# Attention values of two head pairs at once on TensorE, out projections in the steps between, and a reordered VectorE program

## The chip, the cores and the metric

The kernel runs on one core of a Trainium2 chip. A core has five engines that run their own instruction streams and meet at semaphores: TensorE (PE, matmuls and transpositions, with its weight loads shown as PEld), VectorE (DVE), ScalarE (ACT), GpSimd (POOL) and SyncE (SP, which issues most transfers). The metric is the device time of one execution in microseconds.

## What is computed

One decoder layer over 8 batches of 256 rows of width 128, in float32. Self-attention has 16 heads of 64, cross-attention one head over 512 context rows, and the feed-forward block quantises its inputs and weights.

```
x = x + _L0_attn_ref(_layernorm(x, axis=-1), L0_attn_norm_scale, L0_attn_wq, L0_attn_wk, L0_attn_wv, L0_attn_w_out, L0_attn_b_out)
x = x + _L0_xattn_ref(ctx_1024, ctx_1024, _layernorm(x, axis=-1), L0_xattn_Wk, L0_xattn_Wv, L0_xattn_bv, L0_xattn_Wq, L0_xattn_bq, L0_xattn_Wo, L0_xattn_bo)
x = x + _L0_ffn_ref(_layernorm(x, axis=-1), L0_ffn_w1, L0_ffn_b1, L0_ffn_w2, L0_ffn_b2)
...
weights = jnp.einsum('bqhd,bkhd->bhqk', q, kf)
weights = jax.nn.softmax(weights, axis=-1).astype(dtype)
new_vals = jnp.einsum('bhqk,bkhd->bqhd', weights, v).astype(dtype)
out = jnp.einsum('bqhe,hed->bqd', new_vals, w_out) + b_out
```

## The kernel before

The self-attention of a batch is done in eight steps, `j` = 0 to 7, one for each pair of heads. A step of one kind ("first" for batch 0, "mid" for batches 1 to 6 in a hardware loop over two batches at a time, "last" for batch 7) is written out by hand on each engine, in the function `step` of that engine, and semaphores tie the engines together. After the last batch come a tail and the feed-forward block. The order of the work is the order in which the code is written. Step `j` works at several pairs at once:

- TensorE projects queries and keys of pair `j + 3` (`project_qk`, called Q below, 6 matmuls), makes the scores of pair `j + 2` (`scores`, S, 12 matmuls), turns the two probability tiles of pair `j` (`turn_probs`, T0 and T1, 4 transpositions each), multiplies values and turned probabilities of pair `j - 1` (`values`, V, 4 matmuls that the profile records as 8) and projects the output of pair `j - 2` into `acc_bank` (`project_out`, P, 2 matmuls recorded as 4).
- ACT splits Q's result (`split_hi`, writes `q_hi`), takes the exponentials of the first and of the second head (`exps`), and copies V's result into `oT`.
- DVE takes the maxima of the scores (`maxima`, writes `negmax`), copies the two turned tiles into `pT` (`keep_turned`), makes the low part of the split (`split_lo`, `q_lo`), and inverts the row sums (`invert_sums`). GpSimd scales the probabilities (`scale_probs`).

Beside this each step has up to two side tasks, at the places `(j, 0)` and `(j, 1)` of a table. All share one PSUM bank, `side_bank`, so each waits until the one before has been copied out (`side_free`).

```
PLACE = {(0, 0): "W2", (0, 1): "TC", (1, 0): "W1", (2, 0): "W3", (2, 1): "TX", (3, 0): "QX", (3, 1): "TH",
         (4, 0): "SX0", (4, 1): "PX0", (5, 0): "SX1", (5, 1): "PX1", (6, 0): "UX", (6, 1): "OX", (7, 0): "V0"}
```

W0 to W3 and V0 project values, TC turns the context (`cT_hi`, `cT_lo`), TX the normalised rows of the cross-attention (`xn2`, made by DVE; its copies are `x2T_hi` and `x2T_lo`), TH the normalised rows of the next batch (`xn1`; `ht_hi`, `ht_lo`); QX makes the cross queries (`qx_hi`, `qx_lo`), SX0 and SX1 the cross scores (DVE `x_negmax`, then ACT `x_prob`), PX0 and PX1 turn their probabilities (ACT copies them into `x_pT`), UX and OX finish the cross-attention (`uT`, `x_all`). In every step TensorE writes the side task of the first place between Q and S, and that of the second between P and V. ACT takes the copy of the second place's task after the exponentials of the first head and before those of the second.

`turned_bank` is the single bank for T0 and T1, so T1 waits until DVE has copied T0, and T0 until it has copied the T1 before. The scores of step `j` wait until both heads' exponentials of step `j - 1` are out of the two score banks. `residual` in step 1 adds the projected output of the previous batch to its rows; `statistics`, `aggregate` and `normalise` are the three parts of a layer norm, whose inverse root is taken by GpSimd between the last two.

## Time and profile before

| | |
|---|---|
| time before, median of 3 runs | 398.27 us (397.82 to 398.81) |
| profiled execution, its own time | 397.71 us |
| its span (first to last instruction) | 395.9 us |
| TensorE busy | 379.5 us, 96% of the span |
| TensorE weight loads | 286.7 us, 72% |
| DVE busy | 324.5 us, 82% |
| ACT busy | 259.4 us, 66% |
| POOL busy | 163.8 us, 41% |
| granted TensorE clock | 0.999 of full speed |

The span runs from the first to the last instruction; the time of the execution holds 1.8 us more around it. A group of instructions is named by the line that issues it, its engine and what it writes and reads. Matmuls overlap each other, so the duration of one is longer than its distance to the next; a matmul in float32 is recorded as two.

### The profile page before, as it was taken

Reading aid. Unit: us, or ns where it says so; the run is one execution under the profiler, and the core shown is the slowest. Engines: PE = TensorE matmul, PEld = TensorE weight load, DVE = VectorE, ACT = ScalarE, POOL = GpSimd, SP = SyncE. Lnnn points to the kernel's source line nnn. Section 1 sums busy time; section 2 is a strip of 40 time slices with the busy share of each in tenths; the row PEclk is TensorE's granted clock in tenths of the full one; section 3 lists DMA queues with packets and bytes.
Section 4 is the critical chain, followed back from the end, with each engine's and each line's share of the span. In section 5 each row is a group of like instructions: output and inputs, shape, how many; then the busy total and the mean of one; then the engine's idle time right before and its main releaser. Section 6 shows DMA issues by size and latency. Waiting matters only on the chain.

```text
span 395.9 us, 9105 instructions
## 1 busy us (share of the span) xinstructions
PE 379.5 (96%) x3011; PEld 286.7 (72%) x3011; DVE 324.5 (82%) x777; ACT 259.4 (66%) x807; POOL 163.8 (41%) x179
## 2 busy tenths in 40 slices
PE   8999999999999999999999999999999999988975
PEld 8778777777777777777777777777777777766422
DVE  3988779869897889869895989869986998757994
ACT  4976676666667556767676656757675677725674
POOL 3665444524544345425454345444453444501000
PEclk9999999999999999999999999999999999999999
DMA  7500000001000100001000100001000000000003
GB/s 244 142 15 2 2 2 0 3 2 40 2 3 2 40 0 0 0 0 40 0 0 0 40 0 0 0 4 36 0 0 0 26 2 2 0 2 0 2 0 106
DMA packets 12310, 7.50 MB, mean 19 GB/s; under 512 B 1280, under 2 KB 11264, under 8 KB 12288
## 3 DMA queue, kind: packets, MB, share of 16 engines
q1 hardware_dynamic: 11856, 6.69, 5.7%
q10 hardware_dynamic: 432, 0.52, 0.4%
q8 instruction: 13, 0.21, 0.3%
q14 instruction: 9, 0.07, 0.1%
HBM read 6.16 MB, written 1.05 MB: 18 GB/s over the span
## 4 chain that ended last, share of the span: by engine, by line
PE 65%; DVE 18%; issue 10%; ACT 3%; DVEq 1%; POOL 1%; POOLq 0%; ACTq 0%
PE turned_bank L473 13%; PE o_bank L482 12%; PE score L463 12%; PE acc_bank L489 5%; DVE negmax L925 3%; DVE pT L932 3%; PE side_bank L446 3%; PE side_bank L540 3%; PE q_bank L446 3%; PE q_bank L448 3%; PE q_bank L447 3%; DVE h_max L1250 2%; PE side_bank L447 2%; PE side_bank L448 2%; ACT prob L746 2%
## 5 line engine op out<-in xcount | busy, mean ns | idle before, releaser
L1294 POOL TENSOR_TENSOR prob<-prob,rinv 128x512 f32<-128x512 f32 x128 | 132.6, 1044 | 146.6 <-DVE rinv L929 146.6
L746 ACT ACTIVATE prob<-score,negmax 128x256 f32<-128x256 f32 x252 | 117.6, 476 | 71.5 <-DVE negmax L925 69.7
L925 DVE TENSOR_REDUCE negmax<-score 128x2 f32<-128x512 f32 x126 | 85.9, 682 | 27.0 <-PE score L463 25.6
L932 DVE COPY pT<-turned_bank 128x512 f32<-128x512 f32 x124 | 84.2, 679 | 7.0 <-PE turned_bank L473 6.6
L473 PE MATMUL turned_bank<-ident,prob 128*128 128x128 f32 x496 | 81.0, 286 | 1.7 <-DVE pT L932 1.2
L473 PEld LDWEIGHTS turned_bank<-ident,prob 128*128 128x128 f32 x496 | 52.0, 141 | 33.6 <-issue 24.2
L482 PE MATMUL o_bank<-pT,v_sb 128*64 128x256 f32 x512 | 69.4, 392 | 0.6 <-ACT oT L737 0.6
L746 ACT ACTIVATION_READ_ACCUMULATOR prob<-score,negmax 128x1 f32 x252 | 51.3, 203 | 0.0
L482 PEld LDWEIGHTS o_bank<-pT,v_sb 128*64 128x64 f32 x512 | 31.1, 136 | 19.9 <-issue 8.2
L737 ACT ACTIVATE q_hi<-q_bank 128x512 fp32r<-128x512 f32 x63 | 38.2, 606 | 10.9 <-PE q_bank L448 10.0
L917 DVE TENSOR_TENSOR q_lo<-q_bank,q_hi 128x512 fp32r<-128x512 f32 x63 | 42.7, 680 | 0.0
L463 PE MATMUL score<-q_hi 64*128 64x256 f32 x252 | 42.2, 330 | 0.2
L446 PE MATMUL q_bank<-ht_hi,wqk_hi 128*128 128x256 f32 x126 | 40.9, 325 | 0.0
L1285 POOL TENSOR_TENSOR rstd<-veps,ln_pow 128x2 f32<-128x2 f32 x24 | 17.0, 710 | 53.5 <-DVE veps L948 52.8
L489 PE MATMUL acc_bank<-wo_sb,oT 128*128 128x128 f32 x256 | 39.0, 276 | 0.0
L463 PEld LDWEIGHTS score<-q_hi 64*128 64x128 f32 x252 | 23.7, 184 | 18.6 <-issue 15.4
L463 PE MATMUL score<-q_lo,q_hi 64*128 64x256 f32 x252 | 35.6, 277 | 0.0
L463 PE MATMUL score<-q_hi,q_lo 64*128 64x256 f32 x252 | 35.6, 277 | 0.0
L448 PE MATMUL q_bank<-ht_hi,wqk_lo 128*128 128x256 f32 x126 | 35.4, 281 | 0.0
L447 PE MATMUL q_bank<-ht_lo,wqk_hi 128*128 128x256 f32 x126 | 35.3, 280 | 0.0
L489 PEld LDWEIGHTS acc_bank<-wo_sb,oT 128*128 128x128 f32 x256 | 34.1, 191 | 1.0 <-issue 0.4
L737 ACT ACTIVATE oT<-o_bank 128x256 f32<-128x256 f32 x64 | 25.1, 393 | 3.8 <-PE o_bank L482 3.8
(240 smaller groups left out, 622.0 us busy)
## 6 DMA issues: line engine op xcount, KB each, us to landing
c_sb<-in_ctx_dram SPq DMA_DIRECT2D x8, 256.0 KB, 2.9
x_sb<-in_x_dram SPq DMA_DIRECT2D x8, 128.0 KB, 2.6
out_dram<-xn_all SPq DMA_DIRECT2D x4, 256.0 KB, 2.9
big<-in_L_attn_wk_dram ACTq DMA_DIRECT2D x2, 256.0 KB, 4.5
big<-in_L_attn_wq_dram SPq DMA_DIRECT2D x2, 256.0 KB, 5.3
big<-in_L_attn_wv_dram SPq DMA_DIRECT2D x2, 256.0 KB, 5.8
wo_sb<-in_L_attn_w_out_dram SPq DMA_DIRECT2D x1, 512.0 KB, 7.2
w_sb<-in_L_ffn_w_dram SPq DMA_DIRECT2D x2, 256.0 KB, 4.5
```

Of the source, the lines that this page charges most:

```text
L446: nc.tensor.matmul(dst, lhs_hi, rhs_hi, start=True, stop=False)
L447: nc.tensor.matmul(dst, lhs_hi, rhs_lo, start=False, stop=False)
L448: return nc.tensor.matmul(dst, lhs_lo, rhs_hi, start=False, stop=True)
L463: last = nc.tensor.matmul(banks[r][:, t * S:(t + 1) * S], query[rows, parity, 0, t * P:(t + 1) * P], key[rows, parity, 1, :], start=(n == ...
L473: last = nc.tensor.transpose(bank[:, kt * S + t * P:kt * S + (t + 1) * P], prob[:, slot, t, kt * P:(kt + 1) * P], ident[:])
L482: last = nc.tensor.matmul(o_bank[r * E:(r + 1) * E, 0:S], v_sb[:, vp, kt, h * E:(h + 1) * E], pT[:, slots[r], kt, :], start=(kt == 0), sto ...
L489: last = nc.tensor.matmul(acc_bank[:, t * D:(t + 1) * D], oT[:, pair % 2, t * P:(t + 1) * P], wo_sb[:, pair, :], start=(pair == 0 and t == 0),
L737: return nc.scalar.activation(dst, src, ACT.Copy, **kw)
L746: last = nc.scalar.activation(prob[:, slot, t, :], banks[r][:, t * S:(t + 1) * S], ACT.Exp, bias=negmax[:, slot, t:t + 1], scale=1.0, accu ...
L925: nc.vector.tensor_reduce(negmax[:, slot], banks[r][:].rearrange("p (t k) -> p t k", k=S), X_AXIS, ALU.max, negate=True).then_inc(max_done, 1)
L932: nc.vector.tensor_copy(pT[:, slot].rearrange("p k q -> p (k q)"), bank[:]).then_inc(pT_done, 1)
L1294: nc.gpsimd.tensor_tensor(prob[:, slot], prob[:, slot], rinv[:, slot].unsqueeze(2).to_broadcast([P, QT, S]), ALU.mult).then_inc(prob_done, 1)
```

## The change

The values of two pairs are multiplied in one go, in the even steps (pairs `j - 2` and `j - 1`), into the two halves of `o_bank`, and copied to `oT` by one 128x512 copy. The two out projections that belong to them stand in the following odd step. `pT` grows from 4 to 8 slots. On TensorE the second place's side task goes ahead of values or projections only if it is TC or TH; the others (TX, PX0, PX1, OX) come behind them. P of the last pair leaves its place ahead of the scores of step 1. On DVE `split_lo` moves from behind the second maxima to the front of the step, ahead of the side task and the first maxima; `residual` and the normalising of `xn2` move from ahead of the first maxima to behind the second, and `aggregate(2)` in step 7 and `aggregate(1)` in step 1 move later too. On GpSimd the inverse root of step 1 moves behind the first scaling. In the last batch the last context task moves from step 6 to step 7, and after the last step the values of the last two pairs go into two banks.

```diff
-LAST_PLACE[6, 1] = "TL"
+LAST_PLACE[7, 1] = "TL"
...
-        pT = sb("pT", [P, 4, QT, S])
+        pT = sb("pT", [P, 8, QT, S])
...
-            def values(pair, slots, vp):
+            def values(pair, vp, dst):
...
-                        last = nc.tensor.matmul(o_bank[r * E:(r + 1) * E, 0:S], v_sb[:, vp, kt, h * E:(h + 1) * E],
-                                                pT[:, slots[r], kt, :], start=(kt == 0), stop=(kt == QT - 1))
-                last.then_inc(o_raw, 1)
+                        last = nc.tensor.matmul(dst[r * E:(r + 1) * E, :], v_sb[:, vp, kt, h * E:(h + 1) * E],
+                                                pT[:, 2 * (pair % 4) + r, kt, :], start=(kt == 0), stop=(kt == QT - 1))
+                return last
...
-                if cross and j == 1:
-
-                    pe.wait_ge(o_done, g - 1)
-                    project_out(PAIRS - 1)
...
-                if task := side_at(kind, j, 1):
+                task = side_at(kind, j, 1)
+                if task in ("TC", "TH"):
                     side(kind, b, 1 - parity, i, task)
...
+                halves = b * (PAIRS // 2) + j // 2
+                if j % 2 == 0 and not (kind == "first" and j == 0):
+                    wait(pe, o_done, halves - 1)
                     if late(kind, j):
                         pe.wait_ge(pT_done, 2 * g)
-                    slot = 2 * (j - 1) % 4
-                    values((j - 1) % PAIRS, (slot, slot + 1), 1 - parity if j == 0 else parity)
+                    for n in range(2):
+                        last = values((j - 2 + n) % PAIRS, 1 - parity if j == 0 else parity, o_bank[:, n * S:(n + 1) * S])
+                    last.then_inc(o_raw, 1)
+                if j % 2 == 1 and not (kind == "first" and j == 1):
+                    pe.wait_ge(o_done, halves)
+                    if j == 3:
+                        wait(pe, x1_done, b)
...
+                    project_out((j - 3) % PAIRS)
+                    project_out((j - 2) % PAIRS)
+                if task and task not in ("TC", "TH"):
+                    side(kind, b, 1 - parity, i, task)
...
-                if not (kind == "first" and j < 1):
-                    act.wait_ge(o_raw, g)
-                    copy(oT[:, (j - 1) % 2], o_bank[:, 0:S]).then_inc(o_done, 1)
+                if j % 2 == 0 and not (kind == "first" and j == 0):
+                    act.wait_ge(o_raw, b * (PAIRS // 2) + j // 2)
+                    copy(oT[:].rearrange("p n q -> p (n q)"), o_bank[:]).then_inc(o_done, 1)
...
-                if cross and j == 2:
-                    normalise(1, tiles(xn2), tiles(x1_sb), b, xn2_done)
...
+                if ahead(kind, j, 3) and not (kind == "first" and j == 0):
+                    dve.wait_ge(q_hi_done, g + 4)
+                    split_lo((j + 3) % 2, q_banks[(j + 3) % 2])
                 if task := side_at(kind, j, 0):
                     side(kind, b, 1 - parity, task)
-                if cross and j == 1:
-                    residual(b, 1 - parity)
...
-                if ahead(kind, j, 3):
-                    dve.wait_ge(q_hi_done, g + 4)
-                    split_lo((j + 3) % 2, q_banks[(j + 3) % 2])
+                if cross and j == 1:
+                    residual(b, 1 - parity)
+                if cross and j == 2:
+                    normalise(1, tiles(xn2), tiles(x1_sb), b, xn2_done)
```

TensorE in step 4 of a middle batch, from the last scores to T1, where `side_bank<-ident,x_prob` is PX0; before:

```order
L463 MATMUL score<-q_hi,q_lo 128x256 x2
L567 REGISTER_ALU
L473 MATMUL turned_bank<-ident,prob 128x128 x4
L489 MATMUL acc_bank<-wo_sb,oT 128x128 x2
L118 REGISTER_ALU
L536 MATMUL side_bank<-ident,x_prob 128x128 x4
L482 MATMUL o_bank<-pT,v_sb 64x256 x4
L594 REGISTER_ALU
L473 MATMUL turned_bank<-ident,prob 128x128 x4
```

The same place on TensorE in the changed kernel:

```order
L463 MATMUL score<-q_hi,q_lo 128x256 x2
L563 REGISTER_ALU
L473 MATMUL turned_bank<-ident,prob 128x128 x4
L482 MATMUL o_bank<-pT,v_sb 64x256 x8
L118 REGISTER_ALU
L536 MATMUL side_bank<-ident,x_prob 128x128 x4
L595 REGISTER_ALU
L473 MATMUL turned_bank<-ident,prob 128x128 x4
```

The out projection has left the step, and PX0 stands behind eight values matmuls where it stood ahead of four.

VectorE from the end of step 4 to the copy of T0 in step 5 (`x_negmax` belongs to SX1), before:

```order
L932 COPY pT<-turned_bank 128x512
L1056 ISA
L929 RECIPROCAL rinv<-rowsum 128x2
L1007 REGISTER_ALU
L1009 TENSOR_REDUCE x_negmax<-side_bank 128x1
L1073 REGISTER_ALU
L925 TENSOR_REDUCE negmax<-score 128x2
L1075 REGISTER_ALU
L932 COPY pT<-turned_bank 128x512
```

The same place on VectorE in the changed kernel:

```order
L936 COPY pT<-turned_bank 128x512
L1060 ISA
L933 RECIPROCAL rinv<-rowsum 128x2
L1069 REGISTER_ALU
L921 TENSOR_TENSOR q_lo<-q_bank,q_hi 128x512
L1011 REGISTER_ALU
L1013 TENSOR_REDUCE x_negmax<-side_bank 128x1
L1075 REGISTER_ALU
L929 TENSOR_REDUCE negmax<-score 128x2
L1077 REGISTER_ALU
L936 COPY pT<-turned_bank 128x512
```

`q_lo` has come ahead of `x_negmax` and of the maxima. In step 3 it stands in the same way ahead of `qx_lo`.

## Rows read from the trace of the kernel before

**Rows 1.** The page's head: the span, and each engine's busy time (share) xinstructions.

```profile
span 395.9 us, 9105 instructions
...
PE 379.5 (96%) x3011; PEld 286.7 (72%) x3011; DVE 324.5 (82%) x777; ACT 259.4 (66%) x807; POOL 163.8 (41%) x179
```

**Rows 2.** Windows of five middle batches, last line: their length, sums and means.

```profile
sum 218.46, PE 216.88 PEld 166.52 DVE 185.77 ACT 145.42 POOL 99.71; mean PE 43.38 PEld 33.30 DVE 37.15 ACT 29.08 POOL 19.94
```

**Rows 3.** Timeline, TensorE, steps 4 and 5: start, us, instructions merged.

```profile
162.38 0.66 PE L473 MATMUL turned_bank<-ident,prob 128*128 128x128 f32 x4
162.88 0.61 PE L489 MATMUL acc_bank<-wo_sb,oT 128*128 128x128 f32 x4
163.32 0.60 PE L536 MATMUL side_bank<-ident,x_prob 128*128 128x128 f32 x4
163.85 1.08 PE L482 MATMUL o_bank<-pT,v_sb 128*64 128x256 f32 x8
164.87 0.66 PE L473 MATMUL turned_bank<-ident,prob 128*128 128x128 f32 x4
...
167.78 0.66 PE L473 MATMUL turned_bank<-ident,prob 128*128 128x128 f32 x4
```

**Rows 4.** Timeline, TensorE, step 1: Q's last matmuls and W1's first.

```profile
144.17 0.28 PE L447 MATMUL q_bank<-ht_lo,wqk_hi 128*128 128x256 f32 x1
144.28 0.28 PE L448 MATMUL q_bank<-ht_hi,wqk_lo 128*128 128x256 f32 x1
144.96 0.51 PE L446 MATMUL side_bank<-wv_hi,ht_hi 128*128 128x512 f32 x1 [0.40 <-DVE cT_lo L917]
```

**Rows 5.** Narrow windows on one values group: what runs then, with its start.

```profile
119.79 0.27 PE L536 MATMUL side_bank<-ident,x_prob 128*128 128x128 f32 x1
...
119.99 0.44 PE L482 MATMUL o_bank<-pT,v_sb 128*64 128x256 f32 x2
...
120.26 0.60 PE L482 MATMUL o_bank<-pT,v_sb 128*64 128x256 f32 x4
...
120.47 0.60 PE L482 MATMUL o_bank<-pT,v_sb 128*64 128x256 f32 x4
...
120.69 0.39 PE L482 MATMUL o_bank<-pT,v_sb 128*64 128x256 f32 x2
121.01 0.33 PE L473 MATMUL turned_bank<-ident,prob 128*128 128x128 f32 x1
...
121.17 0.38 PE L473 MATMUL turned_bank<-ident,prob 128*128 128x128 f32 x2
```

**Rows 6.** Timeline, ACT, steps 4 and 5.

```profile
164.13 0.59 ACT L737 ACTIVATE x_pT<-side_bank 128x512 f32<-128x512 f32 x1
164.61 0.48 ACT L746 ACTIVATE prob<-score,negmax 128x256 f32<-128x256 f32 x1
...
165.51 0.40 ACT L737 ACTIVATE oT<-o_bank 128x256 f32<-128x256 f32 x1
166.28 0.60 ACT L737 ACTIVATE q_hi<-q_bank 128x512 fp32r<-128x512 f32 x1 [0.38 <-PE q_bank L448]
167.70 0.69 ACT L757 ACTIVATE x_prob<-side_bank,x_negmax 128x512 f32<-128x512 f32 x1 [0.82 <-DVE x_negmax L1009]
```

**Rows 7.** Timeline, DVE, step 5.

```profile
166.97 0.69 DVE L1009 TENSOR_REDUCE x_negmax<-side_bank 128x1 f32<-128x512 f32 x1 [0.65 <-PE side_bank L448]
167.87 0.69 DVE L925 TENSOR_REDUCE negmax<-score 128x2 f32<-128x512 f32 x1 [0.20 <-PE score L463]
168.47 0.69 DVE L932 COPY pT<-turned_bank 128x512 f32<-128x512 f32 x1
```

**Rows 8.** Normalising on DVE: the pair of step 3; all, ns min/median/max.

```profile
156.04 1.31 DVE L957 TENSOR_SCALAR xn<-x_sb,mv,rstd 128x128 f32<-128x128 f32 x2
...
L957 DVE TENSOR_SCALAR xn<-x_sb,mv,rstd x32: 341/627/1077, 6.6 to 355.4; 128x128 f32<-128x128 f32 x32
```

**Rows 9.** Timeline, ACT, last batch: the weights' scaling behind step 1's output copy.

```profile
325.06 1.89 ACT L737 ACTIVATE w_t<-w_sb,w_inv 128x128 f32<-128x128 f32 x5
```

More of the change, by code:

```diff
@@ L574, in step @@
                     turn_probs(2 * j % 8 + 1, turned_in(kind, j, 1))
-                if not (kind == "first" and j < 1):
-                    wait(pe, o_done, g - 1)
-                if j != 1 and not (kind == "first" and j < 2):
-                    if j == 2:
-                        wait(pe, x1_done, b)
-                    if kind == "first" and j == 2:
-                        pe.wait_ge(load_wo, 16)
-                    project_out((j - 2) % PAIRS)
-                if task := side_at(kind, j, 1):
+                task = side_at(kind, j, 1)
+                if task in ("TC", "TH"):
                     side(kind, b, 1 - parity, i, task)
-                if not (kind == "first" and j < 1):
-                    if j == 1:
-                        pe.wait_ge(side_free, side_index(kind, b, "W1"))
+                halves = b * (PAIRS // 2) + j // 2
+                if j % 2 == 0 and not (kind == "first" and j == 0):
+                    wait(pe, o_done, halves - 1)
                     if late(kind, j):
                         pe.wait_ge(pT_done, 2 * g)
-                    slot = 2 * (j - 1) % 4
-                    values((j - 1) % PAIRS, (slot, slot + 1), 1 - parity if j == 0 else parity)
+                    for n in range(2):
[5 more added lines that the diff above has]
+                        wait(pe, x1_done, b)
+                    if kind == "first" and j == 3:
+                        pe.wait_ge(load_wo, 16)
+                    project_out((j - 3) % PAIRS)
+                    project_out((j - 2) % PAIRS)
+                if task and task not in ("TC", "TH"):
+                    side(kind, b, 1 - parity, i, task)
                 if not no_scores:
@@ L622, in _ @@
             over_batches(pe, step)
+            pe.wait_ge(pT_done, B * H - 2)
+            pe.wait_ge(o_done, B * PAIRS // 2 - 1)
+            values(PAIRS - 2, LAST % 2, o_bank[:, 0:S]).then_inc(o_raw, 1)
             pe.wait_ge(pT_done, B * H)
-            pe.wait_ge(o_done, B * PAIRS - 1)
-            values(PAIRS - 1, (2, 3), LAST % 2)
-            project_out(PAIRS - 2)
-            pe.wait_ge(o_done, B * PAIRS)
-            project_out(PAIRS - 1)
+            values(PAIRS - 1, LAST % 2, score_bank[0][:, 0:S]).then_inc(o_raw, 1)
+            for n in range(2):
+                pe.wait_ge(o_done, B * PAIRS // 2 + n)
+                project_out(PAIRS - 2 + n)
             for task in AFTER_LAST:
@@ L796, in step @@
                     exps(1, (2 * j + 5) % 8)
-                if not (kind == "first" and j < 1):
-                    act.wait_ge(o_raw, g)
-                    copy(oT[:, (j - 1) % 2], o_bank[:, 0:S]).then_inc(o_done, 1)
+                if j % 2 == 0 and not (kind == "first" and j == 0):
+                    act.wait_ge(o_raw, b * (PAIRS // 2) + j // 2)
+                    copy(oT[:].rearrange("p n q -> p (n q)"), o_bank[:]).then_inc(o_done, 1)
                 if kind == "last" and j == 1:
@@ L856, in _ @@
             over_batches(act, step)
-            act.wait_ge(o_raw, B * PAIRS)
-            copy(oT[:, (PAIRS - 1) % 2], o_bank[:, 0:S]).then_inc(o_done, 1)
+            for n, bank_o in enumerate((o_bank, score_bank[0])):
+                act.wait_ge(o_raw, B * PAIRS // 2 + n)
+                copy(oT[:, n], bank_o[:, 0:S]).then_inc(o_done, 1)
             for task in AFTER_LAST:
@@ L1057, in step @@
                     invert_sums((2 * j + 3) % 8)
-                if kind == "mid" and j == PAIRS - 1:
-                    aggregate(2, b, *PLAIN_NORM)
                 if kind == "mid" and j == 0:
@@ L1083, in step @@
                     dve.wait_ge(pT_raw, 2 * g + 2)
-                    keep_turned(2 * j % 4 + 1, turned_in(kind, j, 1))
+                    keep_turned(2 * (j % 4) + 1, turned_in(kind, j, 1))
+                if kind == "mid" and j == PAIRS - 1:
+                    aggregate(2, b, *PLAIN_NORM)
                 if more_scores:
@@ L1104, in step @@
                     invert_sums((2 * j + 4) % 8)
+                if cross and j == 1:
+                    aggregate(1, b, *PLAIN_NORM)
                 if not no_scores:
                     dve.wait_ge(pT_raw, 2 * g + 2)
-                    keep_turned(2 * j % 4 + 1, turned_in(kind, j, 1))
+                    keep_turned(2 * (j % 4) + 1, turned_in(kind, j, 1))
                 if kind == "mid" and j == PAIRS - 2:
@@ L1312, in step @@
                     inverse_root(2, b)
-                if cross and j == 1:
-                    inverse_root(1, b)
                 if more_scores:
@@ L1317, in step @@
                     scale_probs((2 * j + 4) % 8)
+                if cross and j == 1:
+                    inverse_root(1, b)
                 if prepare and j == 2:
```

5 lines of the change are left out of this document (3 added, 2 removed).

## The prediction

> **What bounds the kernel now.** I read the page first: TensorE (PE) is busy for 379.5 of 395.9 us and VectorE (DVE) for 324.5 [rows 1]. The windows of five middle batches, cut where the same DVE instruction recurs, give 218.46 us for five, 43.69 each, with PE busy 43.38 of it [rows 2]. A full PE row can still hide waits and switches, so I went to TensorE's timeline and took the distance from one group's start to the next. From here a step is one value of j, S its scores, T0 and T1 its two turnings, V a values group, P an out projection, PX and the like a side task.
>
> In steps 4 and 5 of a middle batch [rows 3], P takes 0.44 (162.88 to 163.32), PX 0.53 when V follows, V 1.02, and T1 0.41 plus Q, SX and S takes us from 164.87 to 167.78, 2.91. The same groups have the same lengths in every middle batch, so I sum them. Without waits a batch comes to 42.75 us; PE therefore waits for about 0.95 in the 43.69. The largest piece is 0.56 before the projection of W1 in step 1: Q's matmuls follow each other at 0.11 to 0.12, but W1 starts 0.68 after Q's last, at 144.96, and the row puts the wait on the DVE copy of the turned context [rows 4]. T1 of step 1 waits another 0.16 for a DVE copy; the rest is five pieces below 0.13. So TensorE's own instructions bound this kernel, with DVE and ScalarE (ACT) so close behind that a chain grown by half a microsecond shows.
>
> **What grouping the values saves.** The 64 values groups use 64 columns of the array; all around them use 128. One group seen instruction by instruction [rows 5]: the last transposition before it starts at 119.79, the next pair would be due 0.11 later by its neighbours' pace but starts at 119.99; the pairs then start at 120.26, 120.47, 120.69, so a pair is worth 0.215, and the first took 0.26; the turning behind starts at 121.01, 0.10 later than a pair's pace would have it; its second transposition follows at 121.17 instead of 0.11 after the first, 0.05 more. In all 0.09 + 0.05 + 0.10 + 0.05 = 0.29 us each time the array goes into the narrow form and out. The change makes four groups of 16 records out of eight groups of 8 in each batch: 4 x 0.29 = 1.17 us less a batch. A double group costs 1.02 + 4 x 0.215 = 1.87. The least gain is nothing, if a switch also occurs between the two halves of a double group (they write other columns of one bank, in the same narrow form, so I take the full value); two P together cost 2 x 0.44. The Trainium skill (TensorEngine Tiling, Key Properties) says that a change of tiling mode drains the engine while a change of tile does not. By that rule the saving is the full one, and the trace agrees at 0.29 a visit.
>
> The other side of the same edit: two output copies of 128x256 become one of 128x512. By ACT's spacings that is 0.26 twice against 0.48 once; it is off PE's path unless something is queued behind it, which is what follows. The DVE reorder puts the aggregate, residual and normalising work behind the two maxima and the context's copy before it; instructions neither appear nor vanish. I count 0.45 of the W1 wait and 0.09 of T1's as recovered, and the small old waits vanish because their places now stand behind larger ones: all 0.95 goes.
>
> **What it makes late.** In an even step the side task of the second place now stands behind 16 records of values instead of behind P: it starts 0.59 + 1.87 = 2.46 after S ends, formerly 0.49 + 0.44. ACT takes that task's copy before the second exponentials, so these, the output copy and the next step's q_hi queue behind it. On DVE q_lo, which waits for q_hi, now stands ahead of the side task and the maxima. I worked the eight steps through with starts and spacings from the rows.
>
> Step 4 to 5, from the start of PX0, with ACT [rows 6] and DVE [rows 7]: x_pT can start at 0.70 (PX itself 0.60 and the array's way out); to the second exponentials 0.48 (164.13 to 164.61); these 0.90 (to 165.51); the wide output copy 0.48, as x_pT has the same shape; q_hi 0.60 and 0.04 to reach DVE; q_lo 0.60; x_negmax 0.69 and 0.04; x_prob 0.79 with its readout and 0.06 until PE sees it. Sum 5.38. PE meanwhile needs 0.49 (PX0), 2.86 (T1 without the way out of values, Q, SX, S), 0.49 (T0) and 0.89 (two P) = 4.73 to the place of PX1. **PE waits 0.65.** Before, q_lo stood behind and x_negmax started as soon as SX ended, at 166.97.
>
> Step 2 to 3. TX needs xn2, which DVE makes after three 0.60 instructions that start when S ends; two undisturbed normalising instructions are 0.34 each (minimum of [rows 8]), and DVE comes 0.27 late out of step 1: xn2 is there at 2.85, PE at 2.46, **0.4 of wait**. From TX: x2T_hi starts at 0.45, exponentials 0.28 later, output copy 0.92 later, q_hi 0.48 later at 2.13. DVE begins normalising the next batch's rows when the second exponentials are out, at about 1.9; the pair lasted 1.31 against 0.68, while GpSimd's scaling and bias add ran beside it [rows 8], so until 3.2; then q_lo 0.60, qx_lo 0.47, 0.06: the side bank is free at 4.3. TH, now directly behind T0, is due at 0.27 + 0.36 + 0.80 + 0.55 + 0.91 + 0.49 = 3.4. **PE waits 0.9**, where before P stood between and the bank came free in time. The Trainium skill (SBUF — State Buffer, SBUF: two separate sides) calls the port pair that DVE and GpSimd share an exclusive lock held for a whole instruction. The 1.31 agrees. By that rule an instruction that finds GpSimd idle isn't held, and the wait would be 0.5.
>
> Smaller ones by the same working: S of step 0 behind the second exponentials of step 7, 0.15; W1 still 0.11; T1 of steps 1 and 7, 0.07 each, since T0 and two P (1.38) are over just before the first pT copy, which starts after 0.70 and ends after 1.38 plus 0.06; SX0 of step 4, 0.14. New waits: 0.65 + 0.4 + 0.9 + 0.54 = 2.5 us.
>
> **The sum.** A batch: -1.17 - 0.95 + 2.5 = +0.4, so 44.1 us instead of 43.7. Six middle batches give +2.3. The first batch has no cross attention: three double groups save 0.9 and T1 and S wait 0.9 (in steps 5 and 3 S is due 2.6 and 3.0 after the last S, and the second exponentials let it go after 3.1): 0. In the last batch ACT scales the feed-forward weights for 1.89 between the exponentials and q_hi of step 1 [rows 9]; q_lo now holds DVE until then, so maxima, xn2 and TX come late by 1.7; with that and the tail, which has both values groups of the last two pairs behind the last turning, I get +1.5. Together +3.8 us, on 397.7 for the profiled run: 401.5; the median of the runs shown is 398.27, 0.6 above that run, which gives **402**.
>
> Bounds of the unknown: the switch saving 0 to 1.17; TH 0.5 to 1.2, PX1 0.4 to 0.9, TX 0.2 to 0.6, the small ones together 0.2 to 0.8. New waits thus 1.3 to 3.5 a batch, the net -0.8 to +1.4, over seven batches -5.6 to +9.8 us.
>
> **Rivals.** (1) The queues catch up and TensorE's saving prevails. For it: DVE and ACT have idle time in most steps (0.65 before x_negmax at 166.97, 0.82 before x_prob at 167.70 [rows 6, 7]), so a late copy may be absorbed. Against it: the two chains above hold no idle time. It decides once new waits are under 2.1 a batch; at 1.4 a batch is 0.7 shorter, seven of them 5 us: 393. With no new wait at all it would be 398.3 - 7 x 2.1 = 383.6. (2) The gains and the waits cancel: 398.3, within 0.3% (1.2 us, about what a measurement of this kernel can tell). (3) The double group still pays for a switch between its halves, so that the change doesn't do what it says: 7 x 1.17 = 8 us more than forecast, 410. Nothing in the trace speaks for it but that no such group exists there.
>
> **Chances.** The forecast's mechanism, ending above 399.5: 0.64. Cancelling within 0.3%: 0.14. Rival 1: 0.19. Rival 3: 0.03. So slower 0.67, same 0.14, faster 0.19. My range is 394.5 to 406: it cuts rival 1 at its stronger half and leaves out rival 3 and the upper end of the bounds.
>
> **What would show it.** Right: values groups of 16 records at 1.87 us; a middle batch of about 44.1; PE idle before side tasks of line 528, 502 and 536 in steps 2, 3 and 5, released by DVE xn2, DVE qx_lo and ACT x_prob, near 0.4, 0.9 and 0.65; q_hi of step 5 starting 2.6 us after PX0. Wrong: batches under 43 with those idle times below 0.3, or values groups of 2.0. The forecast hangs most on ACT's order, which keeps the side copy ahead of the exponentials, and on q_lo's new place; if DVE reaches q_lo with q_hi long done, the PX1 and TH waits fall by up to 0.6 each.

## The result and the profile after

| | before | after |
|---|---|---|
| median | 398.04 us (397.74 to 398.81, 4 runs) | 411.48 us (411.09 to 411.67, 4 runs) |
| span of the profiled execution | 395.9 us | 409.3 us |
| mean of five middle batches | 43.69 us | 45.22 us |

The ratio is 1.0331, with a 95% interval of 1.0316 to 1.0346. The change makes the kernel 13.4 us slower, where I had forecast 3.7. Direction and places were right; the size lay outside my range.

The head of the changed kernel's page, to be held against [rows 1]:

```profile
span 409.3 us, 9116 instructions
PE 376.0 (92%) x3011; PEld 288.6 (71%) x3011; DVE 323.7 (79%) x777; ACT 254.8 (62%) x776; POOL 164.5 (40%) x179
```

TensorE does the same 3011 records in 3.5 us less and is busy for 92% of the span instead of 96%: it works less and waits much more. Next, windows of the changed kernel, cut where UX starts (columns: the stretch, its length, then busy us and count for each engine, then the granted clock, the DMA share and GB/s):

```profile
87.28:132.41 45.13, 42.80 (x355) 33.54 (x354) 36.71 (x89) 28.36 (x93) 19.99 (x22) 1.00 0.04 10
...
313.39:365.60 52.21, 49.06 (x410) 38.22 (x409) 39.81 (x92) 32.28 (x102) 20.19 (x21) 1.00 0.02 6
365.60:409.00 43.40, 33.47 (x181) 18.93 (x179) 32.26 (x91) 23.74 (x44) 2.79 (x4) 0.94 0.08 25
```

Before, the first of these cuts lies at 84.03 us, five batches take 218.45, the stretch up to the last batch's UX 50.16, and 43.3 remain. So the 13.4 us divide into 3.2 ahead of the first cut, 7.7 in five batches, 2.05 up to the last batch's UX and 0.4 behind it. Of the first 3.2, some 2.1 arise in batch 0: the Q that started at 46.43 starts at 48.53.

The waits of TensorE in the changed kernel (us in total, times, longest), largest first:

```profile
PE turned_bank L473 <- DVE pT L936: 6.8, 12, 1.2
PE side_bank L502 <- DVE qx_lo L1003: 5.5, 6, 0.9
PE side_bank L528 <- DVE xn L961: 3.8, 7, 1.0
PE side_bank L536 <- ACT x_prob L760: 2.9, 6, 0.5
```

Three of the four are the forecast's side tasks: TH behind `qx_lo`, TX behind `xn2`, PX1 behind `x_prob`. The first is the one that I had at 0.14 us a batch. It has two large parts. One is in step 2; TensorE's timeline, from the last scores on:

```profile
201.09 0.29 PE L463 MATMUL score<-q_hi,q_lo 64*128 64x256 f32 x2
201.82 0.63 PE L473 MATMUL turned_bank<-ident,prob 128*128 128x128 f32 x4 [0.44 <-DVE pT L936]
202.38 1.95 PE L482 MATMUL o_bank<-pT,v_sb 128*64 128x256 f32 x16
204.78 0.30 PE L528 MATMUL side_bank<-ident,xn 128*128 128x128 f32 x1 [0.46 <-DVE xn L961]
```

S takes 1.42 from start to T0 instead of 0.91: T0 waits for the copy of the turning before it, 0.51 us. TX then waits 0.52. VectorE's timeline ahead of that copy:

```profile
199.77 0.17 DVE L933 RECIPROCAL rinv<-rowsum 128x2 f32<-128x2 f32 x1
199.86 0.23 DVE L949 BATCH_NORM_AGGREGATE mv<-stats 128x2 f32<-128x6 f32 x2
200.12 0.97 DVE L952 TENSOR_SCALAR veps<-mv 128x2 f32<-128x2 f32 x1
201.00 0.68 DVE L936 COPY pT<-turned_bank 128x512 f32<-128x512 f32 x1
```

`veps`, the last instruction of `aggregate(1)`, works on 128x2 elements and takes 0.97 us. GpSimd's timeline has what ran beside it, released by the very reciprocal that stands two instructions ahead:

```profile
200.02 1.04 POOL L1301 TENSOR_TENSOR prob<-prob,rinv 128x512 f32<-128x512 f32 x1 [2.79 <-DVE rinv L933]
```

GpSimd's scaling ends at 201.06 and `veps` at 201.09. The kernel before has one such long `veps` in a batch too, at a place where no copy that TensorE waits for comes late by it:

```profile
135.14 0.97 DVE L948 TENSOR_SCALAR veps<-mv 128x2 f32<-128x2 f32 x1
```

The other large part is in the first batch, where T0 and T1 of step 0 now follow each other and T1 waits until its bank has been copied:

```profile
21.25 0.63 PE L473 MATMUL turned_bank<-ident,prob 128*128 128x128 f32 x4
23.10 0.63 PE L473 MATMUL turned_bank<-ident,prob 128*128 128x128 f32 x4 [1.23 <-DVE pT L936]
```

Step 3, first TensorE, then VectorE:

```profile
207.58 0.66 PE L473 MATMUL turned_bank<-ident,prob 128*128 128x128 f32 x4
209.16 0.44 PE L502 MATMUL side_bank<-ident,xn 128*128 128x128 f32 x2 [0.92 <-DVE qx_lo L1003]
```

```profile
206.72 1.32 DVE L961 TENSOR_SCALAR xn<-x_sb,mv,rstd 128x128 f32<-128x128 f32 x2
207.96 0.68 DVE L921 TENSOR_TENSOR q_lo<-q_bank,q_hi 128x512 fp32r<-128x512 f32 x1
208.56 0.47 DVE L1003 SCALAR_TENSOR_TENSOR qx_lo<-side_bank,qx_bias,qx_hi 128x256 fp32r<-128x256 f32 x1
```

The chain is the one forecast, link by link: a pair of 1.32 for the normalising, then `q_lo`, then `qx_lo`, then TH, 1.08 us late. Step 5, TensorE and then VectorE:

```profile
219.73 1.06 PE L489 MATMUL acc_bank<-wo_sb,oT 128*128 128x128 f32 x8
221.27 0.66 PE L536 MATMUL side_bank<-ident,x_prob 128*128 128x128 f32 x4 [0.48 <-ACT x_prob L760]
```

```profile
219.11 0.69 DVE L921 TENSOR_TENSOR q_lo<-q_bank,q_hi 128x512 fp32r<-128x512 f32 x1 [0.81 <-ACT q_hi L740]
219.72 0.68 DVE L1013 TENSOR_REDUCE x_negmax<-side_bank 128x1 f32<-128x512 f32 x1
```

Two P take 0.89 without a wait, and PX1 starts 1.54 behind the first: 0.65 us of wait. ScalarE's `q_hi` of this step starts at 218.46, 2.56 behind PX0's 215.90, where I had 2.6.

### The profile page after: what moved, and what is told of

It reads as the page before. It is cut to its first block, busy times and chain, and to the rows that moved or that the text cites. A ratio compares the mean times of both kernels' runs of the same rounds, so it can differ in the third digit from the quotient of the medians.

```text
span 409.3 us, 9116 instructions
## 1 busy us (share of the span) xinstructions
PE 376.0 (92%) x3011; PEld 288.6 (71%) x3011; DVE 323.7 (79%) x777; ACT 254.8 (62%) x776; POOL 164.5 (40%) x179
## 4 chain that ended last, share of the span: by engine, by line
PE 53%; DVE 24%; issue 11%; ACT 8%; DVEq 1%; DMA 1%; POOL 1%; POOLq 0%; ACTq 0%
PE o_bank L482 10%; PE turned_bank L473 9%; PE score L463 8%; PE acc_bank L489 4%; DVE pT L936 4%; DVE negmax L929 4%; ACT prob L749 3%; PE side_bank L540 3%; DVE xn L961 2%; DVE h_max L1257 2%; PE side_bank L446 2%; DVE q_lo L921 2%; PE side_bank L536 2%; PE q_bank L446 2%; PE q_bank L447 2%
## 5 line engine op out<-in xcount | busy, mean ns | idle before, releaser
L473 PE MATMUL turned_bank<-ident,prob 128*128 128x128 f32 x496 | 79.0, 282 | 7.0 <-DVE pT L936 6.8
L482 PE MATMUL o_bank<-pT,v_sb 128*64 128x256 f32 x504 | 61.4, 385 | 0.0
L482 PEld LDWEIGHTS o_bank<-pT,v_sb 128*64 128x64 f32 x504 | 33.5, 136 | 18.8 <-issue 5.4
L463 PEld LDWEIGHTS score<-q_hi 64*128 64x128 f32 x252 | 23.9, 184 | 21.2 <-issue 15.7
L489 PE MATMUL acc_bank<-wo_sb,oT 128*128 128x128 f32 x256 | 34.2, 277 | 0.0
L489 PEld LDWEIGHTS acc_bank<-wo_sb,oT 128*128 128x128 f32 x256 | 31.2, 192 | 0.5 <-ACT oT L740 0.4
L933 DVE RECIPROCAL rinv<-rowsum 128x2 f32<-128x2 f32 x128 | 20.2, 158 | 8.4 <-ACT prob L749 6.8
```

What stands on the lines that cost most here:

```text
L463: last = nc.tensor.matmul(banks[r][:, t * S:(t + 1) * S], query[rows, parity, 0, t * P:(t + 1) * P], key[rows, parity, 1, :], start=(n == ...
L473: last = nc.tensor.transpose(bank[:, kt * S + t * P:kt * S + (t + 1) * P], prob[:, slot, t, kt * P:(kt + 1) * P], ident[:])
L482: last = nc.tensor.matmul(dst[r * E:(r + 1) * E, :], v_sb[:, vp, kt, h * E:(h + 1) * E], pT[:, 2 * (pair % 4) + r, kt, :], start=(kt == 0) ...
L489: last = nc.tensor.matmul(acc_bank[:, t * D:(t + 1) * D], oT[:, pair % 2, t * P:(t + 1) * P], wo_sb[:, pair, :], start=(pair == 0 and t == 0),
```

## The experiments

All comparisons are with the kernel before on the same chip (median 398.0 beside the changed kernel, 398.2 to 398.4 beside the others). "Batch" is the mean of five middle batches, from one start of UX to the next.

| kernel | median us | ratio, 95% interval | batch us |
|---|---|---|---|
| after | 411.48 | 1.0316 to 1.0346 | 45.22 |
| after, `q_lo` back | 410.58 | 1.0292 to 1.0326 | 45.45 |
| after, PX0, PX1, OX ahead | 417.03 | 1.0459 to 1.0494 | 46.05 |
| after, aggregate early | 406.83 | 1.0197 to 1.0231 | 44.48 |
| after, most put back but the grouping | 426.92 | 1.0699 to 1.0734 | 47.80 |
| aggregate early, normalising in step 2 | 403.79 | 1.0117 to 1.0151 | 44.04 |
| aggregate early, `q_lo` behind side copy | 403.36 | 1.0108 to 1.0142 | 43.87 |
| both of these | 402.88 | 1.0096 to 1.0130 | 43.82 |
| before, `q_lo` in front | 410.79 | 1.0291 to 1.0325 | 45.33 |
| grouped, `q_lo` by step | 395.74 | 0.9915 to 0.9948 | 43.02 |
| before, context's copy first | 396.73 | 0.9946 to 0.9974 | 43.26 |
| grouped, VectorE order of before | 427.00 | 1.0706 to 1.0754 | 47.88 |
| `q_lo` by step, output copy later | 396.00 | 0.9920 to 0.9953 | 43.03 |

**`q_lo` back.** In the changed kernel, `q_lo` returns behind the second maxima.

```diff
-                if ahead(kind, j, 3) and not (kind == "first" and j == 0):
-                    dve.wait_ge(q_hi_done, g + 4)
-                    split_lo((j + 3) % 2, q_banks[(j + 3) % 2])
...
+                if ahead(kind, j, 3):
+                    dve.wait_ge(q_hi_done, g + 4)
+                    split_lo((j + 3) % 2, q_banks[(j + 3) % 2])
```

> The changed kernel (411.5 us) with one edit undone: DVE takes q_lo behind the second maxima again. My theory (q_lo, waiting for a late q_hi at the head of DVE's step, delays x_negmax, qx_lo and the maxima): the wait of PX1 (0.65 us a batch) goes, that of TH falls from 1.1 to 0.5, the first batch loses 1.5 us of waits, W1 waits 0.4 longer; 402 to 406 us. Rival (the two-step grouping itself costs the time, through the long values group and the wide output copy): less than 1 us of change, 411.

Only 0.9 us came back, and in the trace only the two ends of the program are shorter: a middle batch became 0.23 longer. The wait of PX1 went from 0.65 to nothing and TH's fell from 1.08 to 0.49, as my chains say. But T0's wait in step 2 grew from 0.51 to 1.10, TX's from 0.52 to 0.77, W1's by 0.51, and SX0 waits 0.25 more. Two of TensorE's waits, against 6.8 us in 12 for the first in the changed kernel, and Q's last matmul with W1's first:

```profile
PE turned_bank L473 <- DVE pT L936: 9.6, 10, 1.1
...
PE side_bank L446 <- DVE cT_lo L921: 2.7, 5, 0.6
```

```profile
194.71 0.28 PE L448 MATMUL q_bank<-ht_hi,wqk_lo 128*128 128x256 f32 x1
195.48 0.50 PE L446 MATMUL side_bank<-wv_hi,ht_hi 128*128 128x512 f32 x1 [0.49 <-DVE cT_lo L921]
```

`q_lo` costs where it stands in front (steps 3 and 5) and where it stands behind (steps 0 to 3), about the same. This decided the later runs.

**PX0, PX1 and OX ahead.** TensorE runs these side tasks ahead of values and projections, as before the change.

```diff
-                if task in ("TC", "TH"):
+                if task in ("TC", "TH", "PX0", "PX1", "OX"):
...
-                if task and task not in ("TC", "TH"):
+                if task and task not in ("TC", "TH", "PX0", "PX1", "OX"):
```

> The changed kernel with PX0, PX1 and OX ahead of values and out projections on TensorE, as before; TX stays behind. My theory: x_pT is copied some 1.1 us earlier in step 4, but with q_lo still in front x_prob isn't ready for a PX0 that comes 1.9 us sooner, so PE waits there instead: 409 to 413 us. Rival (the place of the side task alone is what makes ACT's exponentials late): PX waits vanish, 405 to 407 us.

It is 5.5 us slower than the changed kernel, more than either expectation. PX0 now waits 0.78 and PX1 0.85:

```profile
PE side_bank L536 <- ACT x_prob L760: 7.8, 13, 0.7
```

The probabilities come too late for the early place, so the change's order of these tasks is the better one beside an early `q_lo`.

**Aggregate early.** `aggregate(1)` of step 1 follows the residual, ahead of the reciprocal that releases GpSimd. One more reciprocal, of a constant onto an unused tile, stands between the statistics and it.

```diff
                     residual(b, 1 - parity)
+                    nc.vector.reciprocal(spare[:], ln_pow[:])
+                    aggregate(1, b, *PLAIN_NORM)
...
                     invert_sums((2 * j + 4) % 8)
-                if cross and j == 1:
-                    aggregate(1, b, *PLAIN_NORM)
```

> The changed kernel with aggregate(1) of step 1 ahead of the inverted sums, so that no GpSimd scaling runs beside its last instruction (veps, 0.97 us there against 0.17); a 128x2 reciprocal of a constant onto spare room stands between statistics and aggregate. My theory: the second pT copy of step 1 ends 0.5 to 0.8 us earlier, T0 of step 2 no longer waits 0.5 us in seven batches: 407.5 to 409 us. Rival (DVE is late there by its own load, residual and statistics): no change, 411.5 us.

The time fell by 4.6 us, slightly more than expected. VectorE's timeline in this run, at the same place as above:

```profile
197.88 0.23 DVE L950 BATCH_NORM_AGGREGATE mv<-stats 128x2 f32<-128x6 f32 x2
198.14 0.17 DVE L953 TENSOR_SCALAR veps<-mv 128x2 f32<-128x2 f32 x1
...
198.30 0.67 DVE L937 COPY pT<-turned_bank 128x512 f32<-128x512 f32 x1
198.88 0.15 DVE L934 RECIPROCAL rinv<-rowsum 128x2 f32<-128x2 f32 x1
```

And GpSimd's:

```profile
198.46 1.04 POOL L1302 TENSOR_TENSOR prob<-prob,rinv 128x512 f32<-128x512 f32 x1 [3.19 <-DVE rinv L934]
```

The same instruction takes 0.17 instead of 0.97 when GpSimd is idle. T0's wait in step 2 is gone and TX's halved, 0.77 us a batch, which is the 0.74 by which the batch is shorter. The Trainium skill (SBUF — State Buffer, SBUF: two separate sides) says that a VectorE instruction that needs the port pair shared with GpSimd is fully blocked while a GpSimd instruction that started first holds it. The two runs agree for an instruction of 128x2 elements, and add that the reciprocal at 198.88 runs in 0.15 in the midst of GpSimd's scaling: not every small instruction pays.

**Most put back but the grouping.** `q_lo` behind the second maxima, all side tasks ahead of values, `xn2` normalised ahead of step 2's maxima, aggregate early. The residual and `aggregate(2)` keep the places that the change gave them.

```diff
-                if task in ("TC", "TH"):
+                if task in ("TC", "TH", "TX", "PX0", "PX1", "OX"):
...
+                if cross and j == 2:
+                    normalise(1, tiles(xn2), tiles(x1_sb), b, xn2_done)
                 if prepare and j == 3:
...
-                if cross and j == 2:
-                    normalise(1, tiles(xn2), tiles(x1_sb), b, xn2_done)
+                    nc.vector.reciprocal(spare[:], ln_pow[:])
+                    aggregate(1, b, *PLAIN_NORM)
```

> Double values groups and projections in odd steps kept, the rest put back: q_lo behind the second maxima, every side task ahead of values or projections, xn2 normalised ahead of the maxima of step 2, aggregate(1) ahead of the inverted sums. My theory (the order around the grouping costs the time, the grouping saves 1.2 us a batch): 391 to 397 us, below before. Rival (the grouping itself costs): above 405 us.

My theory was 30 us too low. The trace has TX about 2.0 us late in every batch, 1.9 of it with TensorE idle:

```profile
PE side_bank L529 <- DVE xn L962: 13.3, 7, 1.9
```

In the grouped order P of the last pair runs behind T0 of step 1, no longer ahead of its scores. The chain from there over residual, normalising and `xn2` to TX begins that much later, so the side tasks' old places don't fit the new program. Behind each of these pauses TensorE's granted clock falls too: V takes 3.16 us there against 1.88, and TX 0.59 against 0.34, some 1.5 us of the batch. The number is the rival's (above 405), but this run alone doesn't show that grouping costs; the run with `q_lo` by step speaks against it.

**Normalising in step 2.** With the aggregate early, the next batch's normalising follows that of `xn2`.

```diff
-                if prepare and j == 3:
-                    normalise(0, tiles(xn1), tiles(x_sb[:, 1 - parity]), b + 2, xn1_done)
...
                     normalise(1, tiles(xn2), tiles(x1_sb), b, xn2_done)
+                if prepare and j == 2:
+                    normalise(0, tiles(xn1), tiles(x_sb[:, 1 - parity]), b + 2, xn1_done)
```

> The kernel with aggregate(1) early (406.8 us), and the normalising of the next batch's rows moved from the head of step 3 to step 2, behind that of xn2, where DVE and GpSimd both sit idle for a microsecond. Theory A (TH waits 1.2 us a batch because two normalising instructions are held up by GpSimd and stand ahead of q_lo and qx_lo): the wait of TH falls to 0.6, 402 to 404 us. Theory B (TH waits for qx_hi alone, which ACT makes late): the wait stays, 406 to 407 us.

As theory A had it: 3.0 us less, TH's wait 0.67 instead of 1.08. The prediction's other figure for TH, 0.5 if nothing is held, was too low by 0.17: VectorE now stands idle for 0.73 ahead of `q_lo`, until ScalarE's `q_hi` is there. All normalising instructions of one form, here in the changed kernel (busy us, mean ns | idle before):

```profile
L961 DVE TENSOR_SCALAR xn<-x_sb,mv,rstd 128x128 f32<-128x128 f32 x32 | 14.5, 494 | 1.4 <-POOL rstd L1292 1.4
```

and in this run:

```profile
L962 DVE TENSOR_SCALAR xn<-x_sb,mv,rstd 128x128 f32<-128x128 f32 x32 | 9.0, 338 | 1.4 <-POOL rstd L1293 1.4
```

The mean is now the undisturbed length of [rows 8]: nothing holds them in step 2, where GpSimd is idle.

**`q_lo` behind the side copy, and both.** With the aggregate early, `q_lo` stands behind the first place's side work instead of ahead of it; then the same with the normalising in step 2.

```diff
-                if ahead(kind, j, 3) and not (kind == "first" and j == 0):
-                    dve.wait_ge(q_hi_done, g + 4)
-                    split_lo((j + 3) % 2, q_banks[(j + 3) % 2])
                 if task := side_at(kind, j, 0):
                     side(kind, b, 1 - parity, task)
+                if ahead(kind, j, 3) and not (kind == "first" and j == 0):
+                    dve.wait_ge(q_hi_done, g + 4)
+                    split_lo((j + 3) % 2, q_banks[(j + 3) % 2])
```

> The kernel with aggregate(1) early (406.8 us), and q_lo behind the first place's side copy in each step but still ahead of the maxima. Theory A (of q_lo's places only the one ahead of qx_lo and x_negmax costs): the wait of PX1 (0.65) goes and that of TH falls by 0.6, neither comes back elsewhere: 397 to 400 us. Theory B (as where q_lo went back behind the maxima, 410.6 us, the time taken off the side tasks returns at the other places): 404 to 407 us.

> Both of the two edits before together. Theory A: TH waits 0.3, PX1 not at all, a middle batch takes 43.0 us: 394 to 397 us, below the kernel before. Theory B (the grouping itself costs, since the last out projection now comes 1.8 us later in step 1): 400 us or more.

403.4 and 402.9: theory A of both fell. The first lies between its two theories, the second where theory B had it (400 or more), though theory B's cause, the grouping itself, is not shown by that. PX1's wait went to nothing and TH's to about 0.5, but `q_lo` still stood ahead of the maxima and of T0's copy, so that T1 of step 3 starts 0.60 us later behind P than in the changed kernel. TensorE's first wait in the former run, against 3.7 us in 5 waits with the aggregate early alone:

```profile
PE turned_bank L474 <- DVE pT L937: 7.1, 11, 1.2
```

**Before, `q_lo` in front.** Not grouped: in the kernel before, only `q_lo` goes to the head of VectorE's step.

```diff
+                if ahead(kind, j, 3) and not (kind == "first" and j == 0):
+                    dve.wait_ge(q_hi_done, g + 4)
+                    split_lo((j + 3) % 2, q_banks[(j + 3) % 2])
                 if task := side_at(kind, j, 0):
                     side(kind, b, 1 - parity, task)
...
-                if ahead(kind, j, 3):
-                    dve.wait_ge(q_hi_done, g + 4)
-                    split_lo((j + 3) % 2, q_banks[(j + 3) % 2])
```

> The kernel before (398.2 us) with one edit of the change alone: q_lo at the head of DVE's step. Theory A (its place costs only where q_hi comes late, which the grouping brings about through the side copy and the wide output copy): TH and PX1 wait 0.5 and 0.4, W1's wait of 0.56 goes, 398 to 402 us. Theory B (the place costs as much without the grouping): 405 us or more.

This move alone costs 12.4 us in the ungrouped kernel, as theory B had it. Among its waits are the two that I had put down to move and grouping together, PX1's and TH's:

```profile
PE turned_bank L473 <- DVE pT L932: 4.2, 9, 0.9
PE side_bank L536 <- ACT x_prob L757: 3.7, 13, 0.5
PE side_bank L502 <- DVE qx_lo L999: 2.8, 6, 0.5
```

P between T0 and TH, which I took as the cover before the change, is there, and TH waits 0.64 all the same: the cover was the late place of `q_lo`. PX1 waits 0.4. PX0 waits too (0.57), and so does T1 of step 2 (0.44). Neither waits in the changed kernel, so the 12.4 us are not the changed kernel's 13.4 over again.

**`q_lo` by step.** Grouped, aggregate early, normalising in step 2; `q_lo` at the head only in steps 0, 1, 6 and 7, behind `xn2` in step 2, behind the second place's side copy in steps 3 to 5. TensorE's and ScalarE's programs are those of the changed kernel.

```diff
-                if ahead(kind, j, 3) and not (kind == "first" and j == 0):
+                if ahead(kind, j, 3) and not (kind == "first" and j == 0) and j not in (2, 3, 4, 5):
...
                     normalise(1, tiles(xn2), tiles(x1_sb), b, xn2_done)
+                if ahead(kind, j, 3) and j == 2:
+                    dve.wait_ge(q_hi_done, g + 4)
+                    split_lo((j + 3) % 2, q_banks[(j + 3) % 2])
...
                     side(kind, b, 1 - parity, task)
+                if ahead(kind, j, 3) and j in (3, 4, 5):
+                    dve.wait_ge(q_hi_done, g + 4)
+                    split_lo((j + 3) % 2, q_banks[(j + 3) % 2])
```

> Grouping kept, residual early and the first pair's normalising in step 2 (as in the run at 403.8). q_lo heads VectorE's step only in steps 0, 1, 6 and 7; in step 2 it stands behind the normalising of xn2, in steps 3 to 5 behind the second place's side copy. Theory A (each queue wait is local: what the copy's front place costs in step 3's T1 (0.66) and what its back place costs in W1 are avoided where they arise): a period near 42.8 us against 43.7 in the kernel with q_lo behind the side copy everywhere, five middle batches and the last, so 395 to 397. Theory B (a wait taken away comes back within the next step or two, since VectorE is the queue that everything shares): 401 or more. Between 398 and 401 neither.

395.7 us, as theory A had it: 15.7 us below the changed kernel and 2.6 below the one before. The place of `q_lo` alone makes 8 of the 15.7, against the run at 403.8 with the same two other moves. Windows of this run, up to UX of batch 1 and one batch:

```profile
0.00:84.53 84.53, 79.47 (x660) 64.81 (x661) 65.36 (x156) 57.27 (x178) 41.05 (x50) 1.00 0.16 48
...
84.53:127.45 42.92, 42.51 (x355) 33.49 (x354) 35.26 (x90) 28.61 (x94) 19.86 (x22) 1.00 0.04 11
```

VectorE is busy 1.45 us less a batch than in the changed kernel, since `veps` and the normalising are held no more, and 2.75 of the 3.2 us ahead of the first cut are gone as well. TensorE's largest wait, in four places over the whole run, the first batch's among them:

```profile
PE turned_bank L474 <- DVE pT L937: 3.2, 4, 1.2
```

**Before, context's copy first.** In the kernel before, `q_lo` of step 0 goes behind the copy of the turned context.

```diff
-                if ahead(kind, j, 3):
+                if ahead(kind, j, 3) and not (cross and j == 0):
...
                 if task := side_at(kind, j, 1):
                     side(kind, b, 1 - parity, task)
+                if cross and j == 0:
+                    dve.wait_ge(q_hi_done, g + 4)
+                    split_lo((j + 3) % 2, q_banks[(j + 3) % 2])
```

> The kernel before, with q_lo of step 0 in batches 1 to 7 behind the copy of the turned context, nothing else. Theory A (W1 waits 0.56 us a batch for that copy and nothing else is late): seven times 0.4 to 0.56, so 2.8 to 3.9 us less than the kernel before, 394.4 to 395.5. Theory B (q_lo that comes later delays the scores of step 1 by as much): within 1 us of the kernel before.

W1 now starts 0.17 behind Q's last matmul where [rows 4] have 0.68:

```profile
143.90 0.28 PE L448 MATMUL q_bank<-ht_hi,wqk_lo 128*128 128x256 f32 x1
144.07 0.50 PE L446 MATMUL side_bank<-wv_hi,ht_hi 128*128 128x512 f32 x1
```

The batch is 0.43 shorter, 2.2 us over five, but the last stretch is 0.45 longer, since T1 of step 1 in the last batch starts 0.44 later. So 1.6 us came off, less than theory A's 2.8 to 3.9 and more than theory B's 1. Theory A counted seven waits of W1 at up to 0.56. The trace of before has five, in batches 2 to 6, of 0.56 and 0.28 by turns; W1 of batches 1 and 7 doesn't wait.

**Grouped, VectorE order of before.** The last separation: TensorE and ScalarE as changed, VectorE and GpSimd as before.

```diff
+                if cross and j == 2:
+                    normalise(1, tiles(xn2), tiles(x1_sb), b, xn2_done)
...
+                if cross and j == 1:
+                    residual(b, 1 - parity)
                 if more_scores:
...
-                if cross and j == 1:
-                    residual(b, 1 - parity)
```

> TensorE's and ScalarE's order of the changed kernel (values grouped in even steps, projections in odd ones) with VectorE's and GpSimd's order of the kernel before: the residual ahead of the first maxima in step 1, the normalising ahead of the maxima in step 2, q_lo behind the second maxima. Theory A (the grouping moves P of step 7 behind the scores of step 1, so that the residual holds VectorE about 2 us in every batch): 412 to 420. Theory B (the grouping is free or gains its four switches a batch, 1.17 us, and the new VectorE order is what costs): 400 or less.

427.0 us, 7 above theory A and far from theory B. The residual stands ahead of the maxima and needs P of the last pair; T1 waits behind both, 2.6 us:

```profile
206.84 1.09 PE L473 MATMUL turned_bank<-ident,prob 128*128 128x128 f32 x4 [2.59 <-DVE pT L936]
```

So VectorE's old order doesn't fit the grouped program; the residual had to move behind the maxima. In six of the seven batches the granted clock falls behind this pause, and T1, Q and W1 then take 3.42 us instead of the 1.96 of batch 1, where it doesn't. Six times 1.46 is 8.8 us (an estimate); without them the run would be at 418, within theory A.

**Output copy later.** As `q_lo` by step; ScalarE's wide output copy stands behind the next step's `q_hi`.

```diff
                     split_hi((j + 3) % 2, q_banks[(j + 3) % 2])
+                if j % 2 == 1 and not (kind == "first" and j == 1):
+                    act.wait_ge(o_raw, b * (PAIRS // 2) + j // 2)
+                    copy(oT[:].rearrange("p n q -> p (n q)"), o_bank[:]).then_inc(o_done, 1)
```

> As the kernel with q_lo placed by step, and ScalarE's wide copy of the output rows stands behind the next odd step's q_hi instead of ahead of it. Theory A (the chain from the queries to q_hi to q_lo sets when TH and PX1 may start, and the copy of 0.48 us stands in it): 1 to 3 us below the kernel with q_lo placed by step. Theory B (the output rows' bank comes free later, and the next P waits): equal to it or up to 3 us above.

396.0 us and a batch of 43.03: no difference, as theory B allows. With `q_lo` placed by step, 0.48 us in the chain to `q_hi` no longer show in the time.

## Why the prediction was right or wrong

**Direction, and what grouping saves: right.** A double group has 16 records and takes 1.88 us (1.87 forecast), so no switch happens between its halves and rival 3 is out. Summing the unhindered groups of a changed batch gives 41.6 us, which is 43.69 less my 1.17 and 0.95.

**PX1, TX, TH: right in mechanism, nearly right in size.** Measured 0.65, 0.52 and 1.08 against 0.65, 0.4 and 0.9. The normalising pair was indeed held (1.32), and the run with it in step 2 shows what that did. That TX comes so near is in part luck: with the aggregate early it waits 0.27, so my chain for it was too long, and the other half of its 0.52 has a cause that I had not seen.

**The step that failed is the sum of the new waits, "2.5 a batch".** It is 3.56. Of the 1.07 that is missing, 0.51 is T0's wait in step 2, which I had not listed at all: I costed the moved `aggregate` at nothing ("instructions neither appear nor vanish") and did not see that it now stood behind the reciprocal that releases GpSimd's scaling, which held its 128x2 instruction for 0.8 us. The run with the aggregate early shows this: T0's 0.51 goes and 0.26 of TX's wait with it. The rest is my smaller sizes: TH +0.18, TX +0.12, T1 of steps 1 and 7 +0.19 together, W1 +0.11, OX and SX0 +0.11, against S of step 0, which did not wait (-0.15). In six batches this makes some 6.5 us.

**The first batch, "0", cost about 2.1 us.** I had allowed 0.9 for T1 and S. T1 of step 0 alone waits 1.23, and the trace shows more before TH (0.58), S (0.55 and 0.47) and another T1 (0.43). With `q_lo` by step and the two other moves the Q of 48.53 starts at 48.00, so that only 0.5 of the 2.1 is back; T1's 1.2 is still there. The rest of the 2.75 gained ahead of the first UX comes from batch 1.

**The last batch, +1.5, was 2.05**, and 0.4 more came behind it, which goes with a drop of TensorE's clock rather than with the change (below). In the last batch VectorE stands idle for 0.49 ahead of the `q_lo` that waits for ScalarE's scaling, and TX waits 1.1; I had the maxima and TX late by 1.7. Together 6.5 + 2.1 + 1.0 is the 9.6 by which the span missed my sum.

**The bounds were too narrow.** Their upper end, 3.5 a batch, was made of the waits on my list, and 3.56 lies just above it because of the unlisted one. Over seven batches they gave 9.8 us and had nothing for the first batch, against 13.4 measured; the range of 406 left out even the upper part of them.

**A reading that was off.** The 0.56 for W1 [rows 4] is that of every other batch; over the five it is 0.39 on the mean. The sum of all waits, 0.95, came from the mean of five and is not touched.

**Where I had the cause only half.** I treated grouping as the cause and `q_lo` as a link in its chains. The runs separate them: the `q_lo` move alone costs 12.4 us ungrouped, yet taking it back in the grouped kernel returns 0.9. The effects don't add. What the change lacks is a VectorE order that fits its TensorE order; with one, the same TensorE and ScalarE programs run in 395.7 us. Two things were not tried: `q_lo` behind the maxima in every step together with the two other moves (it was there only with the aggregate held, or with more put back), and an ungrouped kernel with its VectorE order sorted as thoroughly. One small move of that kind brought the ungrouped kernel to 396.7, so how much the grouping itself is worth, forecast at 1.17 us a batch, stays open. Why exactly the two uniform places of `q_lo` come out so nearly equal I can show only wait by wait, not by a rule. How much of the first batch's 2.1 us T1's wait is worth by itself was not tried apart.

## What to carry to other kernels

When work is regrouped on one engine, the in-order queues of the others have to be re-sorted step by step: one place for an instruction in every step (always in front, always behind) was wrong in both forms that ran here, and a mixed one was worth 8 us against the front place, the other things equal. List every instruction that a change moves, small ones too, and ask what the neighbouring engine runs at its new time. And sum waits only after going through every bank's hand-over in turn; a wait that isn't on the list isn't in the bounds either.

## What the runs showed of the hardware

A 128x2 instruction of VectorE took 0.97 us beside GpSimd's 128x512 scaling and 0.17 without it, while a 128x2 reciprocal in the midst of that scaling took 0.15, not held. The order of the two, decided by one reciprocal, was worth 4.6 us.

The granted clock fell behind some pauses of TensorE and not behind others like them. In the grouped kernel with VectorE's old order, two windows from the end of such a pause (204.25 to 206.84):

```profile
206.50:208.50 2.00, 1.66 (x8) 1.69 (x9) 1.97 (x8) 1.68 (x8) 0.77 (x2) 0.56 0.00 0
208.50:210.50 2.00, 2.00 (x9) 1.35 (x9) 2.00 (x4) 0.67 (x2) 1.97 (x2) 0.59 0.00 0
```

0.56 and 0.59 of full speed mean that most of these windows ran at 1.2 instead of 2.4 GHz, after 2.6 us in which TensorE did nothing. Q's matmuls follow each other at 0.21 there instead of 0.12. It happened in batches 2 to 7 of that kernel (0.96 on the mean of a batch), but not in batch 1, behind a pause as long:

```profile
64.62 0.63 PE L473 MATMUL turned_bank<-ident,prob 128*128 128x128 f32 x4 [2.60 <-DVE pT L936]
```

```profile
64.60:67.00 2.40, 2.38 (x19) 2.00 (x21) 2.37 (x9) 2.15 (x8) 1.49 (x2) 1.00 0.00 0
```

In the run with most put back it fell behind all seven pauses of 1.9 us. The changed kernel's pauses left its batches at 1.00 (up to 1.2 us in the first batch, 0.92 in the middle ones), but near its end, behind pauses of 1.24 and 0.75 us, the clock also dropped:

```profile
397.00:399.00 2.00, 1.67 (x4) 0.45 (x4) 1.86 (x8) 2.00 (x4) 0.00 (x0) 0.56 0.00 0
399.00:401.00 2.00, 2.00 (x7) 0.75 (x7) 2.00 (x6) 2.00 (x4) 0.00 (x0) 0.59 0.00 0
```

The profiled execution of the kernel before does the same work behind the same two pauses at 1.00, and the feed-forward part is 0.4 us shorter in it. The drop comes and goes without any change: of the four executions of the changed kernel three have a mean granted clock of 0.994 to 0.996 and a span of 409.3 to 409.5 us, the fourth 1.000 and 408.9, and executions of the kernel before differ too, 0.993 in some and 0.999 or 1.000 in others. So one and the same program meets the drop in one execution and not in another. What decides it these runs do not settle.
